# The experts' head: four raw weight slots filled before the stage, the routing table loaded by GpSimd's queue, the first block's rows gathered sooner

## What is computed

```
x = x + attention(layernorm(x), wq, wk, wv, wo)               # causal, 32 heads, 8 KV heads, rotary
x = x + cross(layernorm(x), ctx)                              # per batch: theta, phi, g, softmax, group norm, relu, out_w, + ctx
x = x + experts(layernorm(x))

experts: probs = softmax(x @ Wg); the best 2 of 8 experts for each of 4096 rows
         each expert takes its first C = 1280 rows in order, later ones are dropped
         out[row] += gate * (relu(rows @ w1[e]) @ w2[e])      # w1 512 x 2048, w2 2048 x 512
```

## Time and profile before

| | us |
|---|---|
| median of 3 runs | 2890.52 (2890.28 to 2890.78) |
| the profiled execution's own time | 2891.91 |
| span of its profile | 2889.9 |
| TensorE busy | 2776.0 (96%) |
| VectorE busy | 1260.8 (44%) |
| ScalarE busy | 904.1 (31%) |
| GpSimd busy | 852.5 (30%) |
| mean granted TensorE clock | 0.982 |

### The profile page before, as it was taken

The page is one execution under the profiler, slowest core; times in us unless marked ns, Lnnn a source line. Parts: engine busy times, 40 slices in busy tenths (PEclk is TensorE's granted clock), DMA queues, the critical chain, the costliest instruction groups (busy, mean ns, idle before and its releaser), DMA issues.

```text
span 2889.9 us, 43592 instructions
## 1 busy us (share of the span) xinstructions
PE 2776.0 (96%) x14604; PEld 2144.6 (74%) x14604; DVE 1260.8 (44%) x2281; ACT 904.1 (31%) x1825; POOL 852.5 (30%) x1323
## 2 busy tenths in 40 slices
PE   8989999988999959999999999999999999999998
PEld 6865555547565638888888888888888888888886
DVE  7756777647788844133133133133133123124111
ACT  2126766641565523132122122122122122113110
POOL 4546777631166652012011111111111111111110
PEclk9989999989999979999999999999999999999999
DMA  3101222243122224032032132122122123122110
GB/s 110 44 1 31 49 45 49 50 92 94 54 87 87 79 83 147 16 117 80 13 117 75 29 109 75 37 95 85 37 86 96 41 73 103 41 70 90 44 41 10
DMA packets 97535, 193.76 MB, mean 67 GB/s; under 512 B 22398, under 2 KB 24030, under 8 KB 97392
## 3 DMA queue, kind: packets, MB, share of 16 engines
q1 hardware_dynamic: 75776, 131.77, 15.7%
q0 software_dynamic: 21616, 59.94, 6.7%
HBM read 147.98 MB, written 38.94 MB: 65 GB/s over the span
## 4 chain that ended last, share of the span: by engine, by line
PE 61%; issue 0%; POOL 0%; DVE 0%; ACT 0%; DMA 0%; DVEq 0%; SPq 0%; ACTq 0%; POOLq 0%
PE ex_hid L101 10%; PE ex_hid L103 10%; PE ex_hid L102 10%; PE ex_acc L101 10%; PE ex_acc L103 10%; PE ex_acc L102 10%; PE ex_xb L1867 1%; POOL slot_table_dram L1726 0%; DMA k<-in_w_tiles_dram 0%; DVE ex_w_l L1802 0%; ACT ex_w_h L1767 0%; ACT ex_w_h L1769 0%; DMA slot_table_dram<-last_val,last_slot 0%; POOL out_dram L1749 0%; DVE ex_ys L1810 0%
## 5 line engine op out<-in xcount | busy, mean ns | idle before, releaser
L1835 DVE SCALAR_TENSOR_TENSOR ex_h0l<-ex_hid,ex_h0h 128x512 fp32r<-128x512 f32 (+1 forms) x192 | 115.7, 603 | 632.7 <-ACT ex_h0h L1776 628.1
L1749 POOL DMA_INDIRECT out_dram<-ex_ys,ex_rows_out x80 | 80.0, 1001 | 1009.0 <-DVE ex_ys L1810 996.8
L1835 DVE SCALAR_TENSOR_TENSOR ex_h1l<-ex_hid,ex_h1h 128x512 fp32r<-128x512 f32 (+1 forms) x192 | 115.6, 602 | 563.7 <-ACT ex_h1h L1776 512.4
L1776 ACT ACTIVATE ex_h0h<-ex_hid 128x512 fp32r<-128x512 f32 (+1 forms) x192 | 101.3, 528 | 702.2 <-PE ex_hid L103 702.2
L1776 ACT ACTIVATE ex_h1h<-ex_hid 128x512 fp32r<-128x512 f32 (+1 forms) x192 | 101.4, 528 | 700.5 <-PE ex_hid L103 668.3
L708 DVE TENSOR_REDUCE at_nb<-at_ring 128x2 f32<-128x512 f32 (+1 forms) x384 | 247.0, 686 | 121.5 <-PE at_ring L814 121.5
L101 PE MATMUL ex_acc<-ex_w_h,ex_h1h 128*128 128x512 f32 x640 | 254.2, 397 | 4.5 <-DVE ex_h1l L1835 4.5
L101 PE MATMUL ex_acc<-ex_w_h,ex_h0h 128*128 128x512 f32 x640 | 253.6, 396 | 3.6 <-DVE ex_h0l L1835 3.6
L103 PE MATMUL ex_acc<-ex_w_h,ex_h0l 128*128 128x512 f32 x640 | 250.3, 391 | 0.0
L103 PE MATMUL ex_acc<-ex_w_h,ex_h1l 128*128 128x512 f32 x640 | 250.3, 391 | 0.0
L646 ACT ACTIVATE at_pT<-at_st 128x512 f32<-128x512 f32 x384 | 210.4, 609 | 126.2 <-PE at_st L824 126.2
(11 more groups left out here) (287 smaller groups left out, 5878.7 us busy)
## 6 DMA issues: line engine op xcount, KB each, us to landing
k<-in_w_tiles_dram SPq DMA_DIRECT2D x256, 256.0 KB
x_in<-in_x_dram SPq DMA_DIRECT2D x32, 256.0 KB
act<-at_raw SPq DMA_DIRECT2D x128, 64.0 KB
at_recb<-o_rec_dram SPq DMA_DIRECT2D x16, 512.0 KB
k<-in_x_dram SPq DMA_DIRECT2D x32, 256.0 KB, 2.7
cx_ctx<-in_ctx_dram SPq DMA_DIRECT2D x16, 512.0 KB
out_dram<-cx_res SPq DMA_DIRECT2D x16, 512.0 KB
xn_dram<-cx_prob SPq DMA_DIRECT2D x16, 512.0 KB
```

The lines of the kernel that those rows point to most:

```text
L1749: pool.indirect_dma_start(io["out_rows"][:, :], bass.IndirectOffsetOnAxis(rows_out[:, i:i + 1], 0), ys[:, i, :], None, bounds_check=B * S ...
L1776: act.activation(h[f % 2][0][:, 0:tiles * P], hid[f % 2][:, 0:tiles * P], ACT.Relu)\
L1835: dve.scalar_tensor_tensor(h[f % 2][1][:, 0:tiles * P], hid[f % 2][:, 0:tiles * P], 0.0, f32(h[f % 2][0][:, 0:tiles * P]), ALU.max, ALU.su ...
```

## The change

Raw weight slots: four instead of two, over the whole of `t["k"]`. All four are loaded by SyncE at the end of the cross attention. In the experts' stage two tiles (AHEAD = 2) are split before the first block instead of four, and the rest two turns ahead. The gather buffers get memory of their own. The table is loaded by POOL's queue behind the scatters instead of by SyncE's. In the cross attention `first_rows` stands ahead of `route_place`, and turning, evicting and splitting the gathered rows stands in step n = 16 on each engine instead of after the last step.

```diff
@@ stage_cross, sync
             steps(sp, step)
-            for f in range(2):
+            for f in range(4):
                 sp.dma_start(t["raw"][:, f, 0, :], io["w1_tiles"][f]).then_inc(weights_loaded, 16)
                 sp.dma_start(t["raw"][:, f, 1, :], io["w2_tiles"][f]).then_inc(weights_loaded, 16)
-            sp.wait_ge(weights_loaded, ONE + 64)
+            sp.wait_ge(weights_loaded, ONE + 128)
...
@@ stage_cross, gpsimd, first_rows and step
-                    pool.indirect_dma_start(xin[0][:, i, :], None, io["xn3"][:, :],
+                    pool.indirect_dma_start(xin[0][:, i, :], None, io["xn3"][0:SEALED * CB * S, :],
...
+                if isinstance(n, int) and n == B:
+                    first_rows()
                 if routed and a == 0:
                     route_place(j - 1)
                 if within(n - 1, 0, B):
                     row_root(n - 1, 1 - a)
                 if routed and a == 1:
                     route_count(j - 1)
-                if isinstance(n, int) and n == B:
-                    first_rows()
...
@@ stage_cross, scalar: at the end of step n == B, not after route_exp(groups - 1)
+                if isinstance(n, int) and n == B:
+                    for i in range(TILES[0]):
+                        act.wait_ge(sm["first_turned"], ONE + i + 1)
+                        act.activation(t["first_x"][0][:, :, i * P:(i + 1) * P],
+                                       bank[0][2 + i][:].rearrange("p (k n) -> p k n", k=KD), ACT.Copy)\
+                            .then_inc(sm["first_hi"], 1)
@@ stage_cross, vector: the same place, behind xn3 of the last batch, not after last_group
+                if isinstance(n, int) and n == B:
+                    for i in range(TILES[0]):
+                        dve.wait_ge(sm["first_hi"], ONE + i + 1)
+                        dve.tensor_tensor(t["first_x"][1][:, :, i * P:(i + 1) * P],
...
@@ stage_cross, tensor: ahead of the last batch's x3T transposes, not after the last step
+                if isinstance(n, int) and n == B:
+                    pe.wait_ge(first_gathered, 16 * TILES[0])
+                    for i in range(TILES[0]):
+                        for k in range(KD):
+                            m = pe.transpose(bank[0][2 + i][:, k * P:(k + 1) * P], xin[0][:, i, k * P:(k + 1) * P],
+                                             t["ident"][:])
+                        m.then_inc(sm["first_turned"], 1)
                 if last:
                     for u in range(TPB):
                         pe.wait_ge(sm["xn3"], ONE + TPB * (n - 1) + u + 1)
...
@@ stage_experts
-        RW = 2
+        RW = 4
-        WIDE, AHEAD = max(TILES), 4
+        WIDE, AHEAD = max(TILES), 2
-        xg = [t["k"][:, NT // 2 + KD * r:NT // 2 + KD * (r + 1), :].rearrange("p a c -> p (a c)") for r in range(2)]
+        xg = [s.sb(f"ex_xg{r}", [P, D]) for r in range(2)]
-        filled = s.sb("ex_filled", [P, ST])
+        filled = ys[:, 2, 0:ST]
-        scattered = s.zero_sem("ex_scattered")
+        scattered, table_loaded = s.zero_sem("ex_scattered"), s.zero_sem("ex_table_loaded")
...
@@ stage_experts, sync
-                wait(sp, sm["w_lo"], 2 * (NF * e + f - RW) + 2 if f >= RW else 2 * NF * e)
+                wait(sp, sm["w_lo"], 2 * (NF * e + f - RW) + 2)
...
-            for f in range(RW, AHEAD):
-                load(0, f)
-            sp.wait_ge(scattered, 16 * TOPK * 2 * TPB)
-            sp.dma_start(tab, io["table"][0:SLOTS, :].rearrange("(a b) o -> a (b o)", b=P))\
-                .then_inc(sm["table_loaded"], 16)
-            for f in range(AHEAD, NF):
+            for f in range(RW, NF):
                 load(0, f)
@@ stage_experts, gpsimd, behind the eight scatters
+            pool.wait_ge(scattered, 16 * TOPK * 2 * TPB)
+            pool.dma_start(tab, io["table"][0:SLOTS, :].rearrange("(a b) o -> a (b o)", b=P))\
+                .then_inc(table_loaded, 16)
             pool.wait_ge(sm["slots_ready"], ONE + 1)
@@ stage_experts, scalar (vector likewise with split_lo)
-            for f in range(RW):
-                split_hi(0, f)
-            for f in range(RW, AHEAD):
+            for f in range(AHEAD):
                 split_hi(0, f)
@@ decoder_layer
-        t["raw"] = t["k"][:, 0:NT // 2, :].rearrange("p (r w a) c -> p r w (a c)", r=2, w=2)
+        t["raw"] = t["k"][:].rearrange("p (r w a) c -> p r w (a c)", r=4, w=2)
```

More of the change, by code:

```diff
@@ L1285, in _ @@
             route_exp(groups - 1)
[L1286 to L1290, removed]
         @block.vector
@@ L1430, in step @@
                     xin_lo(n + 2, a)
+                if isinstance(n, int) and n == B:
+                    for i in range(TILES[0]):
+                        dve.wait_ge(sm["first_hi"], ONE + i + 1)
+                        dve.tensor_tensor(t["first_x"][1][:, :, i * P:(i + 1) * P],
+                                          bank[0][2 + i][:].rearrange("p (k n) -> p k n", k=KD),
+                                          f32(t["first_x"][0][:, :, i * P:(i + 1) * P]), ALU.subtract)
             def last_group(g):
@@ L1487, in _ @@
             last_group(groups - 1)
[L1488 to L1492, removed]
         @block.tensor
@@ L1610, in _ @@
             steps(pe, step)
[L1611 to L1616, removed]
             wait_apart(pe, sm["logits_kept"], B, sm["passed_pe"])
@@ L1657, in stage_experts @@
         gathered = [s.zero_sem(f"gathered{r}") for r in range(2)]
-        scattered = s.zero_sem("ex_scattered")
+        scattered, table_loaded = s.zero_sem("ex_scattered"), s.zero_sem("ex_table_loaded")
         rows_loaded, rows_stored = (s.zero_sem("ex_" + n) for n in ("rows_loaded", "rows_stored"))
-        names = ("table_loaded", "table_f", "table_T", "padded", "filled", "slots_ready", "w_hi", "w_lo", "idx_col",
+        names = ("table_f", "table_T", "padded", "filled", "slots_ready", "w_hi", "w_lo", "idx_col",
                  "row_cols", "x_turned", "x_hi", "x_lo", "hidden", "h_hi", "h_lo", "used", "rows_done",
@@ L1813, in table_floats @@
             def table_floats():
-                dve.wait_ge(sm["table_loaded"], ONE + 16)
+                dve.wait_ge(table_loaded, 16)
                 pairs = tab.rearrange("a (b o) -> a b o", o=2)
@@ L1820, in slots @@
                 dve.wait_ge(sm["table_T"], ONE + 1)
-                dve.tensor_scalar(filled[:], xb[:, 0:ST], float(B * S), None, ALU.is_lt).then_inc(sm["filled"], 1)
+                dve.tensor_scalar(filled, xb[:, 0:ST], float(B * S), None, ALU.is_lt).then_inc(sm["filled"], 1)
                 dve.tensor_copy(slot_scatter[:], xb[:, 0:ST])
@@ L1825, in slots @@
                 dve.wait_ge(sm["filled"], ONE + 1)
-                dve.tensor_tensor(slot_gather[:, 0:ST], xb[:, 0:ST], filled[:], ALU.mult)\
+                dve.tensor_tensor(slot_gather[:, 0:ST], xb[:, 0:ST], filled, ALU.mult)\
                     .then_inc(sm["slots_ready"], 1)
@@ L1849, in _ @@
             dve.memset(slot_gather[:], 0).then_inc(sm["padded"], 1)
-            for f in range(RW):
-                split_lo(0, f)
-            for f in range(RW, AHEAD):
+            for f in range(AHEAD):
                 split_lo(0, f)
```

## The result

The changed kernel took 2873.69 us (median of 6 runs, 2868.05 to 2876.54), the one before, beside it, 2889.76 (6 runs, 2883.28 to 2890.78). The ratio is 0.9946, with a 95% interval of 0.9936 to 0.9957: some 15.6 us faster (12.4 to 18.5), where 13.1 were forecast. The forecast of 2877.4 was 3.7 us too high, and the time lies 0.9 under the low end of the range. Of the 3.7, 0.8 is the base: the forecast started from 2890.52 for the kernel before, and beside the changed one it took 2889.76. The profiled execution took 2874.87 us (span 2873.2, granted clock 0.984; before 2891.91, 2889.9, 0.982).

What follows compares the result with a forecast made beforehand. TensorE was taken to lose idle time and half-rate work at the hand-over from cross attention to experts. Gains of 12.6 (head) and 0.5 (stage's end) made 13.1 us, from 2890.52 to 2877.4; 8-in-10 range 2874.6 to 2882.4.

Steps and rivals of the forecast that it cites:

- The stalls at tiles 2 and 4: Start of the experts: TensorE's waits of 3.6 and 4.5 us for hidden values, behind late weight tiles, would go.
- The head, 12.6 us: First expert matmul to outputs of tile 2: 10.75 us for 23.4, about 8.2 of the gain idle time, the rest clock.
- The rival of refilling too late: Experts' first block: refilling two tiles ahead makes steps wait for splits, 12 times, kernel slower, 2893 at 4.1 us steps; chance 0.04.
- The gather's move costs 0.9: Cross attention: POOL's gather ahead of route_place delays row_root, and the last rows' chain down to last_slot, by 0.9 us.
- The end of the stage, 0.5 us: End of the cross attention: stage ends at about 1059.5 for 1060.1, 0.5 us gained (-0.5 to +1).
- the rival of more: Hand-over to the experts: an early clock and an exit freed by the scatters give 2875.5; chance 0.06.
- Table by POOL costs 0: Experts: the table's load behind the scatters on POOL lands at 1081.9, before VectorE wants it, so costs nothing.
- The cover of 2.6 us: Experts: time between the table's landing at 1081.9 and VectorE's need at about 1084.5; 2 if the clock rises early.

Runs made afterwards that it cites:

- slots_old_table: Changed kernel, but SyncE waits for the scatters and loads the table ahead of tile 4, as before; 2880.63 us, 0.9976.
- after_again: Changed kernel unaltered, run once more for the spread; 2872.49 us, 0.9946.
- gather_only: Kernel before with the cross attention's part alone (gather, transposes, eviction and residual sooner), experts' stage as before; 2884.88 us, 0.999.
- pool_order: Kernel before with only POOL's order changed, first_rows ahead of route_place, gathered rows still taken up after the last rows; 2886.32 us, 0.9996.
- pool_tail: Changed kernel with four unread memsets on POOL behind its last cross-stage scatter; 2873.19 us, run once, no ratio.
- late_three: Changed kernel with two of group 6's scatters issued in the experts' stage and only tiles 0 to 2 loaded in the cross stage; 2874.92 us, 0.9958.
- before: The kernel without the change, run beside the changed one; 2889.76 us.
- head_only: Kernel before with the experts' part, the four slots and the table on POOL, the gather left where it was; 2874.93 us, 0.9957.
- ahead4: Changed kernel, splitting four tiles ahead instead of two; 2874.79 us, 0.9951.
- after: The changed kernel in its first runs, against the kernel before; 2873.69 us, 0.9946.
- hold_loads: Changed kernel, SyncE waiting for the eight scatters before it loads tile 6; 2873.79 us, 0.9951.
- table_sp: Changed kernel with tile 6 held for the scatters, and the table loaded by SyncE behind that wait instead of by POOL; 2872.87 us, 0.9956.
- warm_both: Changed kernel with 20 unread matmuls on TensorE, 14 around the last prefix's wait and 6 ahead of the experts; 2871.68 us, 0.9945.
- late_two: Changed kernel with the last two of group 6's scatters issued in the experts' stage behind the eight; 2875.39 us, 0.9962.
- best: Changed kernel with late_two, hold_loads and warm_both in one; 2875.07 us, 0.996.
- best2: late_three with warm_both's 20 unread matmuls, without the held loads; 2875.37 us, 0.996.

## Why the prediction was right, and where it failed

- **The stalls at tiles 2 and 4: right.** Both waits are gone, and slots_old_table shows the second as its own: it needs the table out of its way.
- **The head, 12.6 us: right** (12.4; head 10.97 for 10.75, 11.01 in after_again). The clock rose 5.3 us behind the first expert matmul, where 5 was taken. The rival of refilling too late is refuted by windows at 5.70 of 5.70 and 9.81 of 9.90.
- **The gather's move costs 0.9: right for row_root** (0.8), and at last_slot it can't be told from the spread (0.3 in the first trace, 1.0 in after_again). Its transposes ended 1.5 us before the last rows were ready, as forecast.
- **The end of the stage, 0.5 us: the step that failed.** It came to 3.0 us in the changed kernel, 3.45 and 3.50 in gather_only and pool_order. I took the last scatter's landing (+2.7) and VectorE's residual, 0.4 us apart, for what ended the stage, and 5 us as fixed behind either. So, after the change, I let VectorE's last_group end it at 1059.4, only 0.7 us sooner. That is where it went wrong: each engine has a delay of its own. The next stage starts 6.9 us behind POOL's last instruction (pool_tail), some 2.1 behind VectorE's (late_three), or 4.4 to 4.5 behind the scatter's landing, whichever is latest. Before, VectorE's residual ended at 1059.70; with 2.1 that is 1061.8, no gate beside 1065.27, while 1058.36 + 6.9 is. I had worked out that the scatters start 3.7 us sooner, and gave that only to the rival of more. With 6.9 behind POOL the step would have been 3.7 us and the forecast 2874.2, within 0.6 us of the time. Even that would have missed a part: of the 3.5 us by which POOL was done sooner, the changed kernel's first trace got 3.0, because the landing, at +3.9 instead of +2.7 beside the eight loads, had become the gate.
- **Table by POOL costs 0: right in the end, wrong on the way.** The cover of 2.6 us was used up, and VectorE waited 1.60 (in after_again it didn't wait). The landing taken from the earlier trace rows, 2.7 us from the scatter's issue to the table's, was that of a scatter alone; here 6.2 us lay between the two (5.0 in after_again), among the loads that the change itself brought forward. TensorE lost some 0.1.

Left open: whether the DMAs are what makes POOL's drain last 4.9 us, and what the 4.4 to 4.5 us behind the landing consist of. Nor do the runs order versions within 2 us of each other.

## What to carry to other kernels

When work between two stages is weighed, each engine's last instruction and the next stage's first are to be set side by side, per engine, at more than one hand-over of the trace: a delay that belongs to one engine makes the order of that engine's list the lever. Filled slots only help as far as nothing slow stands ahead of the next refill on the same queue. And a landing time read from a quiet stretch doesn't hold in one which the same change fills with loads.

## What was unexpected of the hardware

- From the end of GpSimd's last instruction to the next stage's first split 6.91 to 6.94 us passed in seven traces (before, gather_only, pool_order, head_only, after_again, ahead4, pool_tail), by whatever instruction it ended; 2.45 us at a hand-over where it had no DMAs. 4.9 us of it is GpSimd's own drain, for 0.1 there. For VectorE it was 2.05 to 2.2.
- Where it was 7.1 to 9.3 us (after, hold_loads, table_sp, warm_both, slots_old_table, late_two, best, best2), the split stood 4.4 to 4.5 us behind the last scatter's landing, which came late while weight loads still ran: 3.6 to 6.2 us from issue to landing, for 2.8 to 3.0 with none under way.
- From the issue of a scatter of 128 rows of 8 bytes to the table's load behind its landing 2.7 us passed in the quiet. With two 256 KB loads a tile beside it 6.2 and 5.0 us passed; 3.2 us when the loads were held back.
